# Two GpSimd additions in front of runs of indirect scatters taken out of a perceiver block with routed experts

## What is computed

```python
x = x + cross_attention(layernorm(x), ctx)         # ctx: 32 x 1601 x 256, 16 heads
x = x + selective_scan(layernorm(x))               # 16 states per channel
h = layernorm(x)                                   # 2048 tokens
scores, idx = top_k(softmax(h @ gate_w.T), 8)      # 64 experts
xbuf = zeros((64, C, 256)).at[e_sorted, pos].set(h[tok_sorted], mode='drop')   # C = 512
y = einsum(silu(xbuf @ w_gate.T) * (xbuf @ w_up.T), w_down)
out = zeros.at[tok_sorted].add(y[e_sorted, safe_pos] * (s_sorted * valid)[:, None])
x = x + out
```

## Time and profile before

| | |
|---|---|
| median of 3 runs | 2489.81 us (2484.97 to 2494.7) |
| the profiled execution's own time | 2486.63 us |
| its span | 2484.9 us |
| mixer phase, from the timeline | 0 to about 1990 us |
| expert phase: first row load to last scatter | 1990 to 2406 us |
| combine phase | to the end |
| PE busy | 2136.3 us (86%) |
| DVE busy | 1786.6 us (72%) |
| ACT busy | 1432.3 us (58%) |
| POOL busy | 674.2 us (27%) |

### The profile page before, as it was taken

One profiled execution on the slowest core, in us unless ns is written; L12 is line 12 of the kernel. 1 busy time (PEld: TensorE's weight loads), 2 busy tenths in 40 slices (PEclk: granted clock), 3 DMA queues, 4 the chain that ended last, 5 costly groups with the idle time before them and its releaser, 6 DMA issues. The chain is left out here.

```text
span 2484.9 us, 55791 instructions
## 1 busy us (share of the span) xinstructions
PE 2136.3 (86%) x21320; PEld 1461.4 (59%) x21320; DVE 1786.6 (72%) x3776; ACT 1432.3 (58%) x2948; POOL 674.2 (27%) x708
## 2 busy tenths in 40 slices
PE   5999999999999999999999999999995089899940
PEld 3666666566666666666666666666663067666730
DVE  4557777878777778787777878787777655555538
ACT  1667666767676667676666667676765144444410
POOL 1002030312222130303030303121220447766650
PEclk9999999999999999999999999999996589999975
DMA  6486662313132323132232333231310156555647
GB/s 202 165 285 231 201 237 76 82 66 83 68 84 76 73 80 85 66 92 89 60 97 52 97 84 79 70 82 67 84 53 34 43 178 187 174 177 181 185 144 270
DMA packets 132950, 294.14 MB, mean 118 GB/s; under 512 B 22139, under 2 KB 89383, under 8 KB 126544
## 3 DMA queue, kind: packets, MB, share of 16 engines
q1 hardware_dynamic: 114256, 255.89, 33.6%
q0 software_dynamic: 18432, 34.69, 3.9%
HBM read 165.40 MB, written 108.27 MB: 110 GB/s over the span
## 5 line engine op out<-in xcount | busy, mean ns | idle before, releaser
L623 PE MATMUL W<-sb_ident,sb_probs 128*128 128x128 f32 (+1 forms) x3328 | 487.6, 282 | 59.8 <-issue 19.5
L783 ACT ACTIVATE sb_probs<-S,sb_negmax 128x1604 f32<-128x1604 f32 x256 | 409.5, 1600 | 224.0 <-DVE sb_negmax L948 221.7
L775 ACT ACTIVATE sb_probsT<-W 128x384 f32<-128x384 f32 (+1 forms) x1024 | 476.1, 514 | 72.1 <-PE W L623 66.9
L623 PEld LDWEIGHTS W<-sb_ident,sb_probs 128*128 128x128 f32 (+1 forms) x3328 | 366.9, 140 | 189.5 <-issue 93.8
L948 DVE TENSOR_REDUCE sb_negmax<-S 128x1 f32<-128x1604 f32 x256 | 465.9, 1820 | 1.5 <-PE S L613 0.3
L596 PE MATMUL W<-sb_wkv_in,sb_ctx 128*128 128x256 f32 (+1 forms) x1664 | 434.0, 405 | 26.7 <-DVE sb_K_lo L932 13.9
L586 PE MATMUL W<-sb_ctx,sb_wkv_in 128*32 128x401 f32 x4096 | 410.6, 503 | 2.5 <-DVE sb_V L942 2.5
L596 PEld LDWEIGHTS W<-sb_wkv_in,sb_ctx 128*128 128x128 f32 (+1 forms) x1664 | 306.7, 194 | 99.3 <-ACT sb_probsT L775 33.0
L767 ACT ACTIVATE sb_K_hi<-W,sb_pair_cols 128x401 fp32r<-128x401 f32 x256 | 153.0, 598 | 336.8 <-PE W L586 259.0
L932 DVE SCALAR_TENSOR_TENSOR sb_K_lo<-W,sb_pair_cols,sb_K_hi 128x401 fp32r<-128x401 f32 x256 | 161.9, 633 | 223.4 <-ACT sb_K_hi L767 221.5
L1279 POOL DMA_INDIRECT y_scratch<-sb_ys,sb_places x256 | 258.3, 1009 | 112.3 <-issue 91.6
(11 more groups left out here) (181 smaller groups left out, 2819.7 us busy)
## 6 DMA issues: line engine op xcount, KB each, us to landing
sb_ctx<-ctxT SPq DMA_DIRECT2D x32, 1604.0 KB, 7.7
xe_scratch<-sb_none SPq DMA_DIRECT2D x32, 1088.0 KB, 12.5
sb_xg<-xe_scratch SPq DMA_DIRECT2D x64, 544.0 KB
sb_BC<-bc_scratch SPq DMA_DIRECT2D x32, 1024.0 KB, 6.3
sb_Q_hi<-sb_q_hi SPq DMA_DIRECT2D x128, 128.0 KB, 4.4
sb_Q_lo<-sb_q_lo SPq DMA_DIRECT2D x128, 128.0 KB, 5.8
y_scratch<-sb_none SPq DMA_DIRECT2D x16, 1024.0 KB
sb_rows<-y_scratch SPq DMA_DIRECT2D x16, 1024.0 KB, 7.5
```

Of the source, the lines that this page charges most:

```text
L623: ins = pe.transpose(W[0:keys_in(t), at * P:(at + 1) * P], probs[n % 2][:, t * P:t * P + keys_in(t)], ident[:])
L775: act.activation(probsT[k][n % (k + 1)][:, 0:wide], ring[bank_of("T", G, k)][:, 0:wide], ACT.Copy)\
L783: act.activation(probs[n % 2][:].rearrange("p (c k) -> p c k", c=QUADS), scores_of, ACT.Exp, bias=negmax[:, slot:slot + 1], accum_out=den[ ...
```

## The change

The addition into `pause_p` and its wait go from the mixer's `scatter`; the addition into `pause_e` and its wait go from the expert phase's POOL turn. The first indirect transfer of each run now stands directly behind the waits that the addition had. Two semaphores and two columns go with them. Nothing else is moved.

```diff
             def scatter(p):
 
                 if p == 0:
                     pool.wait_ge(xe_clear, 16 * CLEARS)
                 pool.wait_ge(routed, p + 1)
-                pool.tensor_tensor(pause_p[:], neg_half[:], neg_half[:], ALU.add).then_inc(idx_seen, 1)
-                pool.wait_ge(idx_seen, p + 1)
                 for t in range(TOPK):
                     pool.indirect_dma_start(
...
                 pool.wait_ge(places_up, e + 1)
                 for m in range(2):
                     pool.wait_ge(y_up[m], e + 1)
-                pool.tensor_tensor(pause_e[:], ident[:, 0:1], ident[:, 0:1], ALU.add).then_inc(places_seen, 1)
-                pool.wait_ge(places_seen, e + 1)
                 for c in range(CT):
                     pool.indirect_dma_start(
```

More of the change, by code:

```diff
@@ L233, in mixer_phase @@
         iota_e = sb("iota_e", [P, E])
-        pause, pause_q, pause_p = (sb(n, [P, 1]) for n in ("pause", "pause_q", "pause_p"))
+        pause, pause_q = (sb(n, [P, 1]) for n in ("pause", "pause_q"))
         neg_half = sb("neg_half", [P, 1])
@@ L336, in mixer_phase @@
         scattered = sem("scattered")
-        idx_seen = sem("idx_seen")
         xe_clear = sem("xe_clear")
@@ L1183, in expert_phase @@
         places = [sb(f"places{n}", [P, CT], U32) for n in range(4)]
-        pause_e = sb("pause_e", [P, 1])
         wgu = [sb(f"wgu{n}", [P, DT, 2 * FF]) for n in range(2)]
@@ L1216, in expert_phase @@
         places_up = sem("places_up")
-        places_seen = sem("places_seen")
         block = ctx.enter_context(nc.Block())
```

## The result

The change takes 2507.31 us, median of 7 runs (2500.84 to 2512.48), beside 2489.81 (2484.93 to 2496.02) for the kernel before in the same comparison: ratio 1.007, 95% interval 1.0049 to 1.0091. It is slower by 17 us, where I forecast 17 us less. All runs of my own met three other chips, on which the kernel before takes 2424 to 2426 us. The same change ran on one of these three, and there it is 2.4% **faster**; the other two ran kernels made from it or from the kernel before.

What follows compares the result with a forecast made beforehand. POOL was taken as the slowest loop of the expert phase in most turns, 6.16 us per run; gains of 11.0 + 4.6 + 0 + 1.8 = 17.4 us off the median 2489.81 gave 2472 us, range 2444 to 2489.

Steps and rivals of the forecast that it cites:

- (1): Expert phase: a run of transfers on POOL loses 0.76 us, from 6.16 to 5.40.
- (2): Expert phase: the bound moves to PE's turns, 5.96 us with its own 29 us of delays kept; gain 11.0 us.
- rival C: Expert phase: denser PE work brings further slow turns at the lower clock, 1.59 us each, making it slower; chance 0.05.
- rival A: Expert phase: PE's own delays go as well, so the gain is 40 us and the time 2449; chance 0.17.
- (3): End of the expert phase: POOL without backlog shortens the 21.05 us from expert 63's start to the last transfer; gain 4.6.
- (4): Mixer's last scatters: 0.7 us from the last pair's run and 1.1 from the one before; gain 1.8 us.
- (5): The mixer's 14 other scatters: POOL saves 1 to 1.6 us each but is mostly idle, so the gain is 0.

Runs made afterwards that it cites:

- h1: The change, with each expert's 12 pairs of gate and up products made twice; 2536.55 us in one run.
- The paced kernel: The change, with PE also waiting in each turn for its expert's places; 2409.73 us, ratio 0.9938, repeated at 2409.64 and 2412.63 us.
- e4: The change, with the last two of each expert's four scatters left out; 2354.06 us, ratio 0.971.

## Why the prediction was wrong

On the first chip it had the wrong sign, and on the other chip that ran the change it would have been too cautious (58 us gained against my 17). By its steps:

**(1) A run on POOL loses 0.76 us: nearly right where the waits had been met, wrong where they had not.** In the first case the expert phase's first transfer started 1.00 us behind the end of the one before, with the addition between them, and now starts 0.30 to 0.48 behind it; a run takes some 5.5 us on the other chips, where it shows, against my 5.40. In the second case only 0.28 us are saved, 0.86 for 1.14. I had no row for that case and put it with the first. It doesn't turn the sign: where POOL waits for `ys`, it isn't the bound.

**(2) The bound moves to the 5.49 us turn of PE: right. PE's own delays stay as they are: wrong, and this is the step that turned the sign.** On the first chip the slow turns went from 12 to 35, those of PE's own making from 9 to 35, and the phase grew by 48 us where I took 11 off. The effect is that of rival C, to which I gave 0.05: 23 more slow turns, 2.1 us for each if all of it is theirs (48.2/23), against my 1.59. I had priced only the lower clock; the late turns, which come at a clock of 1.00, cost 3.2 us each (57.0/18). The row that I set against C, the mixer with PE 89% busy at 0.96, was a row of other work and no evidence for this phase; I had named the row that spoke for it, that PE was slow in some 22 turns for no reason that the waits showed, and then carried those delays over as a constant. An unexplained 29 us deserved a chance on either side.

On the other chips the same step was wrong in the opposite direction. There nearly all slow turns of the kernel before are POOL's doing (31.3 of the 34.5 us over 5.49 stand in turns in which `sg` came late behind ACT's copy), so taking the addition out gave 28 us, between my 11 and the 40 of rival A.

**Why PE slows down on the first chip is not settled.** What is shown: on that chip PE's results are late while its clock still reads 1.00, and the lower level follows for the next turn; the same program on another chip has no turn in which they are late at 1.00; with PE at 100% on a third (h1) there is none either. What was only argued: that the landed rows, which held ACT's copy back for 99.2 us, had paced PE on that chip, and that it runs into the slow turns once nothing does. The paced kernel was made for this and met no such chip. A rival is as open: that the scatters themselves hold PE up there, more so when they stand closer. For it: in the mixer the late results stand beside the runs of scatters and are missing in the pair without one. Against it as the whole cause: in the expert phase POOL's scatters filled more of the time before the change than after it, and the late turns were fewer. e4 tests it only on a chip without slow turns. Nor can the runs tell a property of the first chip from its state at the time, since no later run met it. It also stays open whether the mixer's edit alone would gain on the first chip; its 19 us there, with the expert phase as before, would give 2489.81 - 18.9 = 2471, an estimate. The Trainium skill (TensorE: Matmul & The Clock Gate, Part 1: The HAM clock gate) says that activity releases the throttle, and by that the change should have had fewer slow turns. The first chip's rows went the other way (PEclk 0.98 before, 0.92 with the change); those of h1, 360 us of work at 1.00, agree.

**(3) The tail: right.** 4.0 us on the first chip, 6.6 on the other one, 4.6 forecast; the last scatter ends 17.0 us behind expert 63's start on both, 16.4 forecast.

**(4) The mixer's last scatters, 1.8 us: too high for the last one.** It waits for a fresh `sc_idx`. With the addition its first transfer started 1.06 us behind DVE's write, without it 0.79: 0.27 us gained on either chip, where I counted 0.7. What the run before it gave is not to be told apart from (5).

**(5) The other scatters of the mixer are worth 0: wrong.** They gave 1.55 to 1.7 us per pair, some 20 us. I took POOL's 1602 us of idle time as cover. On the other chips POOL's products had a neighbour that they block, DVE's scan; on the first chip the gain lies in PE's late results beside the scatters. A scan of 4.63 us stood in my own, where a free one takes 1.23, and I read it as DVE's work.

## What to carry to other kernels

An engine that is 27% busy over the whole span can still be the slowest loop of one stage, and its small steps can be on the path of a stage in which it idles for 80% of the time: look at what its neighbours do while it works, above all for an instruction that takes two or four times its usual time. Where an engine has slow turns that no wait explains, do not carry them over as a constant when the pace changes: give both directions a chance. And a gain of one or two per cent should be measured on more than one chip; here its sign differed between two.

## What the runs showed of the hardware

Two chips can differ in one part of a program and not in another: a pair of the mixer without scatters takes 110.8 us on both, with eight scatters beside it 117.9 on the first and 113.35 on the others, and the change has 35 turns over 6.9 us on the first and two on the other that ran it. TensorE's results can be late while the granted clock reads 1.00: two halves of a transpose came 1.46 us apart instead of 0.44. The profile shows that only in the engines that wait. A scan that is blocked by GpSimd shows as busy, 3.02 us for 1.23. An indirect scatter of 128 rows costs GpSimd 0.97 us and 0.30 between two. Behind a fresh result of GpSimd's own it starts after 0.78 us, behind a fresh result of DVE after 0.86 (`ys`) or 0.79 (`sc_idx`), and where its waits have long been met after 0.15 to 0.48.
